# Self attention of a decoder layer: who turns the probabilities and the row tiles

## The reference

```python
def _L0_attn_ref(q, k, v, scale_factor, dropout_p):      # q (4, 1024, 512); k, v (1, 2048, 512)
    b, s, d = q.shape
    step = s // 4
    scale = q[:, ::step].reshape(b, -1)                  # (4, 2048)
    qk = jnp.einsum('bsd,btd->bst', q, k)
    softmax_qk = jax.nn.softmax(qk * scale[:, None, :], axis=-1)
    return jnp.einsum('bst,btv->bsv', softmax_qk, v)
x = x + _L0_attn_ref(_layernorm(x, axis=-1), L0_attn_k, L0_attn_v, ...)
```

## Time and profile before

| | us |
|---|---|
| median of 3 runs | 3876.82 |
| lowest, highest | 3873.74, 3878.27 |
| span of the profiled execution (its own time) | 3891.2 |
| TensorE busy | 3788.4 (97%) |
| VectorE, ScalarE, GpSimd busy | 2395.0, 1432.7, 1534.5 |

### The profile page before, as it was taken

One profiled execution on the slowest core, in us unless ns is written; L12 is line 12 of the kernel. 1 busy time (PEld: TensorE's weight loads), 2 busy tenths in 40 slices (PEclk: granted clock), 3 DMA queues, 4 the chain that ended last, 5 costly groups with the idle time before them and its releaser, 6 DMA issues. The chain is left out here.

```text
span 3891.2 us, 63669 instructions
## 1 busy us (share of the span) xinstructions
PE 3788.4 (97%) x19001; PEld 2532.2 (65%) x19161; DVE 2395.0 (62%) x6222; ACT 1432.7 (37%) x1793; POOL 1534.5 (39%) x860
## 2 busy tenths in 40 slices
PE   8999999999999899999999999999999999999998
PEld 7888888888877444544444444544444777777776
DVE  6544444444458688888888788878887533433135
ACT  3111222233224455455545555445555221222332
POOL 1000000000013667766677666766665222312234
PEclk9999999999999999999999999999999999999999
DMA  4001000145555322222112222222111433328579
GB/s 157 32 32 32 32 32 32 44 172 178 191 179 186 94 57 55 57 57 46 35 38 57 58 57 58 54 57 55 33 36 49 151 126 132 114 92 278 185 263 332
DMA packets 223177, 381.89 MB, mean 98 GB/s; under 512 B 17544, under 2 KB 102056, under 8 KB 222892
## 3 DMA queue, kind: packets, MB, share of 16 engines
q1 hardware_dynamic: 192876, 301.34, 26.7%
q0 software_dynamic: 14752, 49.29, 3.5%
q10 hardware_dynamic: 15264, 27.79, 1.9%
HBM read 229.71 MB, written 148.66 MB: 97 GB/s over the span
## 5 line engine op out<-in xcount | busy, mean ns | idle before, releaser
L1103 DVE CUSTOM_DVE_ANT_0 xf_unread<-xa_mx_ps,mask_q 128x402 bf16<-128x402 f32 x1984 | 1036.0, 573 | 290.3 <-PE xa_mx_ps L1096 156.7
L1726 ACT ACTIVATE probs<-xa_scores 128x1024 f32<-128x1024 f32 (+1 forms) x416 | 417.5, 1024 | 417.0 <-PE xa_scores L1600 371.6
L1726 ACT ACTIVATE xa_probs<-xa_scores 128x1024 f32<-128x1024 f32 (+1 forms) x416 | 417.3, 1024 | 397.8 <-PE xa_scores L1600 355.1
L1561 POOL TENSOR_TENSOR xa_sums<-xa_sums,xa_probs 128x1024 f32<-128x1024 f32 x220 | 519.7, 2383 | 18.1 <-POOL xa_sums L1561 15.7
L1561 POOL TENSOR_TENSOR xa_sums<-xa_sums,probs 128x1024 f32<-128x1024 f32 x220 | 519.3, 2381 | 18.9 <-POOL xa_sums L1561 15.3
L1600 PE MATMUL xa_scores<-mask_t,ident_b 128*128 128x512 bf16 (+1 forms) x1505 | 499.7, 387 | 5.3 <-issue 0.2
L1096 PE MATMUL xa_mx_ps<-xa_kp,queries 96*128 96x402 f32 x1024 | 364.2, 418 | 0.8
L1096 PE MATMUL xa_mx_ps<-xf_kp,queries 96*128 96x402 f32 x960 | 341.5, 418 | 0.4
L1594 PE MATMUL xa_scores<-queries,xf_kp 97*128 97x512 f32 (+1 forms) x832 | 284.2, 423 | 16.3 <-ACTq L1748 8.2
L1096 PEld LDWEIGHTS xa_mx_ps<-xa_kp,queries 96*128 96x128 f32 x1024 | 181.7, 189 | 172.2 <-DVE xf_maxima L1103 111.6
L1594 PE MATMUL xa_scores<-queries,xa_kp 97*128 97x512 f32 (+1 forms) x832 | 284.7, 423 | 1.8 <-ACT probs L1726 1.8
(11 more groups left out here) (415 smaller groups left out, 7388.0 us busy)
## 6 DMA issues: line engine op xcount, KB each, us to landing
bridge_rows<-sorted_in SPq DMA_DIRECT2D x78, 256.0 KB
sorted_out<-ex_made ACTq DMA_DIRECT2D x78, 256.0 KB
queries<-qT_high SPq DMA_DIRECT2D x30, 512.0 KB
xf_kp<-kT_high SPq DMA_DIRECT2D x16, 800.5 KB, 12.4
xa_kp<-kT_high SPq DMA_DIRECT2D x16, 800.5 KB
rows<-in_ctx SPq DMA_DIRECT2D x16, 768.0 KB, 5.1
values<-cxl_v SPq DMA_DIRECT2D x48, 256.0 KB
kT_high<-cxl_kT_high SPq DMA_DIRECT2D x12, 768.0 KB, 4.0
```

The source lines that it names most:

```text
L1103: return dve.tensor_tensor_reduce(out=unread[slot % 2][:, :], in0=scores[:, 0:MKEYS], in1=mask_q[:, half * QB + qt, MFIRST[kb]:MFIRST[kb] ...
L1561: pool.tensor_tensor(sums[pr][:, :, :], left[pr][:, :, :], right[pr][:, :, :], ALU.add).then_inc(pool_added, 1)
L1726: act.activation(prob[ring][pr][0:keys, :, :], scores[pr][0:keys, :, :], ACT.Exp, scale=SCALE).then_inc(exped, 1)
```

## The change

The transposes of probabilities and row tiles leave TensorE. `prob` is turned by VectorE in squares of 32x32: strip i of 32 queries stays on its 32 partitions, key position k within a square goes to the partition. The turned squares are written over `scaled`. SyncE then moves them in sixteen transfers of 32 partitions x 512 words (`move`) from SBUF to SBUF, into `prob`, so that key block a comes onto partition block a. ScalarE and GpSimd (in place of VectorE) split from there, reading runs of 32 words. The row tile is turned by VectorE into `spare`, stored to DRAM (`turned_n`) and loaded back in four transfers (`move_n`). Exp of the next tile waits for the low part of all four groups, since `prob` is read until then; scaling of the next tile waits for the sixteen transfers. The first tile's probabilities and row tiles 0 and 1 stay as they were. In the last tile nine of the fifteen groups of the next stage now come ahead of weighing. Scales are loaded one batch at a time. The diff, cut, with eight leading spaces taken off:

```diff
+SQUARE = 32
+QB = P // SQUARE
+MOVED = 16 * QB * QB
...
+prob_by_key = prob.rearrange("p j (c a k) -> p a (j c) k", a=QB, k=SQUARE)
+squares = scaled.rearrange("p a (c q) -> p a c q", q=SQUARE)
+raw_pT = prob.rearrange("p i (c q) -> p c i q", q=SQUARE)
...
+normed_by_row = normed[:, :].rearrange("p (c a k) -> p a c k", a=QB, k=SQUARE)
+n_squares = spare[:, :].rearrange("p (a c r) -> p a c r", a=QB, r=SQUARE)
+raw_nT = normed[:, :].rearrange("p (i c r) -> p c i r", i=QB, r=SQUARE)
...
-pT_ps = [ps(f"pT_ps{i}", [P, KB, P]) for i in range(2)]
+k_ps = [ps(f"k_ps{i}", [P, KB, P])[:, :, :] for i in range(2)]
 o_ps = ps("o_ps", [P, D])
-k_ps = [pT_ps[0][:, :, :], pT_ps[1][:, :, :], o_ps[:, :].rearrange("p (c n) -> p c n", n=P)]
+first_ps = list(k_ps)
+k_ps.append(o_ps[:, :].rearrange("p (c n) -> p c n", n=P))
...
+def wait_moved(eng, t):
+    eng.wait_ge(p_in, MOVED * t)
+
 GROUPS_W = len(weights) * DC
 LAST_GROUPS = GROUPS_W + FULL
+AHEAD = GROUPS_W - FULL
...
+        def move(t):
+            sp.wait_ge(p_turned, t)
+            for a in range(QB):
+                for i in range(QB):
+                    sp.dma_start(prob[a * SQUARE:(a + 1) * SQUARE, i, :],
+                                 scaled[i * SQUARE:(i + 1) * SQUARE, a, :]).then_inc(p_in, 16)
+
+        def move_n(t):
+            sp.wait_ge(turned, t + 3)
+            sp.dma_start(turned_n, spare[:, :]).then_inc(n_out, 16)
+            sp.wait_ge(n_out, 16 * (t - 1))
+            for a in range(QB):
+                sp.dma_start(normed[a * SQUARE:(a + 1) * SQUARE, :].rearrange("k (i n) -> k i n", n=P),
+                             turned_n[:, a * P:(a + 1) * P].rearrange("(i k) n -> k i n", k=SQUARE)).then_inc(n_in, 16)
...
+        load_scale(1)
+        for t in range(2):
+            if t > 0:
+                load_add(t)
+                store(t - 1)
             load_norm(t + 3)
-            load_add(t + 1)
+            move_n(t + 2)
+            move(t + 1)
+            load_scale(t + 2)
+        with sp.Fori(0, tiles - 5) as t:
+            load_add(t + 2)
             store(t + 1)
+            load_norm(t + 5)
+            move_n(t + 4)
+            move(t + 3)
         sp.wait_ge(scaled_to, NB * (tiles - S // P) + NB + 1)
         for w, weight in enumerate(weights):
             sp.dma_start(scale[:, w, :, :], weight.rearrange("(r p) n -> p r n", p=P)).then_inc(weights_in[w], 16)
-        for t in (tiles - 2, tiles - 1):
+        for t in (tiles - 3, tiles - 2, tiles - 1):
             load_add(t)
-            if t == tiles - 1:
-                sp.wait_ge(exped, tiles + 2)
-                sp.dma_start(opening.rows[:, 0, 0:FULL, :],
-                             context[0][0:FULL * P, :].rearrange("(r p) n -> p r n", p=P)).then_inc(rows_in, 16)
-                sp.wait_ge(p_turned, NB * tiles + NB + 1)
-                sp.dma_start(opening.rows[:, 1, 0:FULL, :],
-                             context[0][FULL * P:2 * FULL * P, :].rearrange("(r p) n -> p r n", p=P)).then_inc(next_rows_in, 16)
-            store(t)
+            store(t - 1)
+            if t == tiles - 3:
+                move_n(t + 2)
+            if t < tiles - 1:
+                move(t + 1)
+        wait_moved(sp, tiles - 1)
...
+        def low_p(t):
+            for j in range(NB):
+                mine = slice(j * KB, (j + 1) * KB)
+                pool.wait_ge(pT_high, NB * t + j + 1)
+                pool.tensor_tensor(pT[1][:, mine, :].rearrange("p c (i q) -> p c i q", q=SQUARE), raw_pT[:, mine, :, :],
+                                   words(pT[0][:, mine, :]).rearrange("p c (i q) -> p c i q", q=SQUARE),
+                                   ALU.subtract).then_inc(pT_low, 1)
...
+        pool.sem_inc(pT_low, NB)
+        for t in range(B + 1):
+            step(t + 2)
+            if t > 0:
+                low_p(t)
+            if 0 < t < B:
+                scale_step(t)
+        with pool.Fori(0, tiles - 3 - B) as t:
+            step(t + B + 3)
+            low_p(t + B + 1)
+        low_p(tiles - 2)
+        low_p(tiles - 1)
...
(TensorE)
         def tile(t, ahead):
-            if ahead >= 1:
-                for j in range(NB - 1):
-                    score(t + 1, j)
-            turn_p(t, 0)
-            turn_p(t, 1)
-            if ahead >= 1:
-                score(t + 1, NB - 1)
-            if ahead >= 2:
-                turn(t + 2)
+            first = isinstance(t, int) and t == 0
+            for j in range(NB) if ahead >= 1 else ():
+                if first and j == NB - 1:
+                    turn_first_p(0)
+                    turn_first_p(1)
+                score(t + 1, j)
+            for n in range(AHEAD) if ahead == 0 else ():
+                turn_last(n)
             for j in range(NB):
                 weigh(t, j)
-                if j + 2 < NB:
-                    turn_p(t, j + 2)
-                for n in range(FULL) if ahead == 0 else ():
-                    turn_last(FULL * j + n)
-            for n in range(FULL * NB, LAST_GROUPS) if ahead == 0 else ():
+                if first and j + 2 < NB:
+                    turn_first_p(j + 2)
+                if ahead == 0 and AHEAD + j < GROUPS_W:
+                    turn_last(AHEAD + j)
+            for n in range(GROUPS_W, LAST_GROUPS) if ahead == 0 else ():
                 turn_last(n)
 
...
(ScalarE)
+        def high_moved_n(t):
+            act.wait_ge(scored, NB * t)
+            act.wait_ge(n_in, 16 * QB * (t - 1))
+            act.activation(nT[0][:, :, :].rearrange("p c (i r) -> p c i r", r=SQUARE), raw_nT,
+                           ACT.Copy).then_inc(nT_high, 1)
...
-            act.wait_ge(p_turned, NB * t + 1 + NB)
+            act.wait_ge(pT_low, NB * (t + 1))
...
+                wait_moved(act, t)
+            mine = slice(j * KB, (j + 1) * KB)
+            act.activation(pT[0][:, mine, :].rearrange("p c (i q) -> p c i q", q=SQUARE), raw_pT[:, mine, :, :],
+                           ACT.Copy).then_inc(pT_high, 1)
...
         def tile(t, ahead):
-            high_p(t, 0)
-            high_p(t, 1)
-            if ahead >= 2:
-                high_n(t + 2)
-            for j in (2, 3):
-                high_p(t, j)
-                for n in range(FULL) if ahead == 0 else ():
-                    high_last(FULL * (j - 2) + n)
-            for n in range(2 * FULL, LAST_GROUPS) if ahead == 0 else ():
+            for n in range(AHEAD) if ahead == 0 else ():
+                high_last(n)
+            if isinstance(t, int) and t == 0:
+                high_first_p(0)
+                high_first_p(1)
+                high_moved_n(t + 2)
+                high_first_p(2)
+                high_first_p(3)
+            else:
+                for j in range(NB):
+                    high_p(t, j)
+                if ahead >= 2:
+                    high_moved_n(t + 2)
+            for n in range(AHEAD, LAST_GROUPS) if ahead == 0 else ():
                 high_last(n)
...
(VectorE)
+        def turn_n(t):
+            dve.wait_ge(normal, t + 3)
+            if isinstance(t, int) and t == 2:
+                dve.wait_ge(v_low_pool, POOL_V)
+            else:
+                dve.wait_ge(n_out, 16 * (t - 2))
+            dve.transpose(n_squares, normed_by_row).then_inc(turned, 1)
...
             if j == 0:
-                dve.wait_ge(exped, t + 2)
+                if isinstance(t, int) and t <= 1:
+                    dve.wait_ge(exped, t + 2)
+                else:
+                    wait_moved(dve, t - 1)
...
+        def turn_p(t):
+            dve.wait_ge(exped, t + 3)
+            dve.transpose(squares[:, :, :, :], prob_by_key[:, :, :, :]).then_inc(p_turned, 1)
...
             if ahead >= 2:
                 normalize(t + 2)
+                turn_n(t + 2)
             if ahead >= 1:
                 for j in range(NB - 1):
                     scale_block(t + 1, j)
                     next_scales(t, j)
-            low_p(t, 0)
-            low_p(t, 1)
+            first = isinstance(t, int) and t == 0
+            for j in range(2) if first else ():
+                low_first_p(j)
             if ahead >= 1:
                 scale_block(t + 1, NB - 1)
                 row_max(t + 1)
             if ahead >= 2:
-                low_n(t + 2)
+                low_moved_n(t + 2)
             next_scales(t, NB - 1)
-            for j in (2, 3):
-                low_p(t, j)
-                for n in range(FULL) if ahead == 0 else ():
-                    low_last(FULL * (j - 2) + n)
-            for n in range(2 * FULL, NB * FULL - FULL) if ahead == 0 else ():
+            for j in range(2, NB) if first else ():
+                low_first_p(j)
+            if ahead >= 1:
+                turn_p(t + 1)
+            for n in range(AHEAD) if ahead == 0 else ():
                 low_last(n)
             add(t)
-            for n in range(NB * FULL - FULL, LAST_GROUPS) if ahead == 0 else ():
+            for n in range(AHEAD, LAST_GROUPS) if ahead == 0 else ():
                 low_last(n)
 
...
```

(70 more changed lines are left out.)

19 lines of the change are left out of this document (9 added, 10 removed).

## The result

The changed kernel takes 3907.69 us (median of 4 runs, 3903.11 to 3911.29) against 3875.28 before: a ratio of 1.008 (95% interval 1.0064 to 1.0097). It is slower by 0.8%; 3813 was forecast.

What follows compares the result with a forecast made beforehand. TensorE's own instruction list was taken to bound the self attention stage: 66.7 us off it, less 0.65 at the start and 2.4 at the end, gives 63.6 us gained and 3813.2 us; 8 in 10 range 3806 to 3852.

Steps and rivals of the forecast that it cites:

- Edit 1: Exp, then VectorE's turning of 128x2048 by squares of 32: turning taken as 2.3 us, between 2.0 and 4.6.
- Rival 4: VectorE's squares take 4.6 us, putting ring (a) at 20.5 and ring (b) at 21.6: 3821 us; chance 0.08.
- Edit 2: SyncE's sixteen transfers of turned probabilities: 0.44 us an issue, 7.0 us in all, plus 1.7 us for the last to land.
- M: Move time of the sixteen transfers, issues plus last landing: taken as 8.7 us, bounds 6.7 and 17.
- rival 1: Move is longer, ring (a) binds from M = 12.7; with M = 13.7 a tile takes 23.2 us, total 3851; chance 0.14.
- ring (a): Per-tile loop of last scale, maximum, exp, turn, move, four scales: 9.5 + M = 18.2 us; 21.5 in tiles 1 to 4.
- ring (b): Per-tile loop of exp, turn, move, high part, four low parts: 10.6 + M = 19.3 us.
- rival 2: Move over 14.9 us makes tiles slower than before; at M = 17, 26.5 us a tile, about 3950; chance 0.09.
- Edit 4: Other VectorE and SyncE work: VectorE's load unchanged, row tile's chain free until the sixteen issues take over 8.8 us.
- ring (c): Per-tile loop of SyncE with the row tile: 13.4 us + the issues = 20.4 us, under 22.1.
- Edit 3: Splitting probabilities from SBUF: ScalarE's high parts 0.62 us each, GpSimd's low parts 1.3 us, from 1.2 up to 2.6.
- Rival 3: GpSimd slow on runs of 32 words: 2.6 us a part gives 3885 us, 2.1 gives 3825; chance 0.09 together.

Runs made afterwards that it cites:

- row store first: Changed kernel with only SyncE's order changed, the row tile's store to DRAM issued ahead of the three other transfers: 3840.62 us, ratio 0.9924.
- late loads: Changed kernel with the 1 MB loads of scales and weights moved behind the row tile's four loads, one a tile: 3895.5 us, ratio 1.0055.
- two queues and late loads: Changed kernel with two queues, row store first and late loads together: 3808.00 us, ratio 0.983.
- two queues: Changed kernel with eight of the sixteen transfers issued by ScalarE right after exp, eight by SyncE: 3814.09 us, ratio 0.9845.

## Why the prediction was wrong

- **TensorE's list** (66.7 us off it, 22.12 us a tile): right. It is 22.13 in every variant in which TensorE binds, 22.55 with one group put back.
- **Edit 1**, turning: 2.31 us where 2.3 was taken, a guess from the maximum that held. The Trainium skill (VectorE: DVE Perf Modes, "The three transpose paths") would have had 5.0 by an estimate from its 311 ns for 128x128; the measurement decides. Rival 4 is out.
- **Edit 2**, the failed term. I took 0.44 us an issue, from loads out of DRAM; from SBUF to SBUF it is 0.627, 10.0 us for sixteen in place of 7.0. The kernel with DRAM as source shows that my rows were right for what they were, and the wrong kind. The landing of 1.7 was 2.0 by the median, and M = 11.4, still below the 12.7 of rival 1. So in the steady tiles rings (a) and (b) did not bind, and rivals 1 and 2 did not happen; but ring (b), 10.6 + 11.4 = 22.0, was only 0.1 us from it. The 7.9 us a megabyte of my bound is 7.5 by its own figures (18 / 2.4); nothing rests on it.
- **Edit 4 and ring (c)**, the failed step. I wrote that the row tile's chain costs nothing until the sixteen issues take over 8.8 us. They take 10.0, and by my own formula the tile would have been 13.4 + 10.0 = 23.4. It is 24.7, since I took the store's landing from a kernel where nothing stood ahead of it in the queue: with its issue 2.5 us against 4.33, behind two loads and a store of 256 KB; the four loads gave 0.6 us back (3.22 for 3.8). I gave this ring no chance of its own. In the steady tiles both errors were needed for the loss: with issues of 0.457 us and the slow store tiles 6 to 27 average 22.16 us (source in DRAM), with issues of 0.627 and the store first 22.29.
- **What a late tile costs.** The ring gives 24.7 to 25.0 us; tiles 6 to 27 average 24.86. Single tiles, from addition to addition, lie between 22.2 and 27.7 us. In the long ones TensorE, after idling, ran at half clock for a while, as here (columns as above); the ring does not contain TensorE, and the next tile takes it up again.

```profile
583.05 0.80 PE L47 MATMUL sa_o_ps<-sa_v_high,sa_pT_high 128*128 128x512 f32 x1 [2.85 <-POOL sa_pT_low L306]
...
569.50:597.20 27.70, 24.85 (x96) 0.88 0.35 92
597.20:619.40 22.20, 22.20 (x98) 1.00 0.36 98
```

- **Tiles 1 to 5** were costed at nothing and are 10.6 us longer than before; **tiles 28 to 30** are 10.7 longer. In tiles 28 to 30 the store of the row tile stands behind 3 MB of weights and lands after 9.8 us. The late loads show that the 1 MB loads were the cause there, and of half of the excess in tiles 1 to 5. For the other half the prediction had ring (a) at 21.5 us there, with 5.7 us of VectorE's work on scales and M = 8.7; with 7.7 us (130.93 to 138.64 in the changed kernel) and M = 11.4 it is 26.2.
- **The last tile**: I forecast 2.4 us for start and end. With two queues and late loads the last addition starts 36.0 us after the last score (715.7 to 751.70) against 30.1 before (782.43 to 812.57): 5.9 more. Weighing starts 1.5 us later than I worked out, and the half clock lasts some 10 us (731.7 to 742.0), not 3.5.
- **Edit 3**: right in the steady tiles. A low part takes 1.30 us, and runs of 32 words cost nothing. Rival 3 is out. But I named the low part of the row tile as the only work on VectorE that GpSimd could disturb, and overlooked the normalization of the scales: 0.90 to 1.58 us beside GpSimd's low parts in place of 0.54.

The sum, 3813, comes close to what two queues measured (3814), in part by luck: the gain over the kernel before was forecast at 63.6 us and is 57.6 there, from a lower median before (3871.65). With the row store first and the late loads too the stage itself is 60.9 us shorter. As built it was held by one queue that does everything in turn.

## What to carry to other kernels

When work moves from the engine that binds to DMAs, write out the ring through the queue that issues them, with every issue and every wait in it, and give it a chance of its own. Take the price of an issue from a transfer of the same kind of source and destination, and the landing of a store from what stands ahead of it in the queue. A queue that waits for a landing between two sets of issues should send other work out first; a second queue halves the rest.

## What the runs showed of the hardware

- In a series of sixteen transfers into SBUF an issue on SyncE takes 0.627 us with SBUF as source, whether for 32 or 128 partitions and 16 or 64 KB, and 0.457 us with DRAM as source (32 partitions, 64 KB). A single store from SBUF to DRAM is issued in 0.35 to 0.46 us. ScalarE's queue takes 0.66 (SBUF to SBUF), at the same time as SyncE's and without slowing it. The Trainium skill (DMA: Bandwidth & Descriptors, the table of where the 2 us go, in the section on the anatomy of a transfer issued by GpSimd) gives some 50 ns for the sequencer's dispatch alone. The whole issue in these traces is nine to thirteen times that, and no run here shows how it divides.
- A 256 KB store to DRAM lands in 2.0 us with only the 64 KB strips issued ahead of it, in 4.4 (median) behind three transfers of its size, and took 9.8 behind three of 1 MB and two of 256 KB.
- VectorE's transpose in squares of 32 in fp32 takes 2.31 us for 128x2048, with a source in runs of 32 words, and 0.71 for 128x512; a maximum over 128x2048 takes 2.29.
- VectorE's normalization of 128x512 within SBUF (subtract and multiply) takes 0.54 us alone and 0.90 to 1.58 us while GpSimd subtracts with both inputs in SBUF; four of GpSimd's subtractions take 5.5 us there in place of 5.0.
- In the changed kernel a wait of TensorE of 2.46 us (until 408.82) was followed by a clock of 1.00, and one of 2.85 us (until 583.05) by half of it for a while.
